# Attention in fp32: the weights of a step's two key blocks added before the products with ones

## The reference

```python
scores = jnp.einsum('bhqd,bhkd->bhqk', qn, kn) / jnp.sqrt(jnp.asarray(hd, x.dtype))
scores = jnp.where(causal, scores, jnp.finfo(scores.dtype).min)
w = jax.nn.softmax(scores, axis=-1)
a = jnp.einsum('bhqk,bhkd->bhqd', w, v)
```

## Time and profile before

| | before |
|---|---|
| median of 3 runs | 2315.25 us (2311.72 to 2317.13) |
| the profiled execution, its own time | 2315.28 us |
| its span | 2313.6 us |
| PE busy | 2164.0 us, 94% |
| DVE busy | 1176.7 us, 51% |
| ACT busy | 809.5 us, 35% |
| POOL busy | 734.2 us, 32% |
| mean granted TensorE clock | 0.969 |

### The profile page before, as it was taken

How to read it: one execution, slowest core, us unless ns; L and a number is a source line. 1 busy time by engine, 2 the same in 40 slices (tenths; PEclk the granted TensorE clock), 3 DMA queues, 4 the chain that set the end, 5 groups by cost and what they waited for, 6 DMA issues and landing times. The chain is left out here.

```text
span 2313.6 us, 36853 instructions
## 1 busy us (share of the span) xinstructions
PE 2164.0 (94%) x14056; PEld 1685.2 (73%) x14056; DVE 1176.7 (51%) x2747; ACT 809.5 (35%) x1607; POOL 734.2 (32%) x612
## 2 busy tenths in 40 slices
PE   6999996599999999999697999999999999999998
PEld 3777774377777777776475888888888888888887
DVE  5999997666667676663695222222212212222212
ACT  3333332056665666666485111111111111111111
POOL 1676776212222213222401742222222222222221
PEclk8999998589999999999898999999999999999999
DMA  6122222637566575741785422121111212121111
GB/s 237 55 104 96 93 98 109 151 94 165 142 149 158 134 164 129 164 109 49 219 303 188 127 78 69 51 69 55 56 45 51 69 57 71 51 69 55 50 33 55
DMA packets 175604, 244.00 MB, mean 105 GB/s; under 512 B 20604, under 2 KB 99580, under 8 KB 174936
## 3 DMA queue, kind: packets, MB, share of 16 engines
q1 hardware_dynamic: 173176, 235.56, 35.6%
q0 software_dynamic: 1216, 3.16, 0.5%
q10 hardware_dynamic: 1056, 3.15, 0.3%
HBM read 131.69 MB, written 59.26 MB: 83 GB/s over the span
## 5 line engine op out<-in xcount | busy, mean ns | idle before, releaser
L1384 DVE TENSOR_TENSOR f_gu<-f_psU,f_silu 128x512 f32<-128x512 f32 x128 | 88.6, 692 | 705.1 <-PE f_psU L1454 705.1
L1000 ACT ACTIVATE b_probT<-b_psB 128x512 f32<-128x512 f32 (+1 forms) x640 | 317.0, 554 | 171.6 <-PE b_psB L864 169.4
L933 DVE TENSOR_REDUCE b_top<-b_psA 128x2 f32<-128x1024 f32 (+2 forms) x320 | 284.6, 902 | 154.1 <-PE b_psA L841 154.1
L1340 POOL TENSOR_SCALAR f_wd_hi<-f_wd 128x512 fp32r<-128x512 f32 x128 | 84.0, 656 | 712.9 <-PE f_psD L1437 712.9
L1360 ACT ACTIVATE f_silu<-f_psG 128x512 f32<-128x512 f32 x128 | 76.5, 598 | 504.8 <-PE f_psG L1454 504.8
L864 PEld LDWEIGHTS b_psB<-b_stack 98*128 98x128 f32 x1280 | 184.2, 191 | 73.1 <-issue 51.6
L864 PE MATMUL b_psB<-b_stack 98*128 98x256 f32 (+1 forms) x1280 | 219.1, 292 | 6.0 <-ACT b_probT L1000 3.7
L1452 PE MATMUL f_psG<-f_hT_hi,w_hi 128*128 128x512 f32 x512 | 200.2, 391 | 12.2 <-DVE f_hT_lo L1378 12.2
L1355 ACT ACTIVATE f_gu_hi<-f_gu 128x512 fp32r<-128x512 f32 x128 | 80.9, 632 | 364.5 <-DVE f_gu L1384 364.5
L841 PE MATMUL b_psA<-b_stack 96*128 96x512 f32 (+3 forms) x768 | 185.0, 371 | 23.5 <-DMA b_stack<-b_halves 18.3
L1454 PE MATMUL f_psG<-f_hT_lo,w_hi 128*128 128x512 f32 x512 | 199.9, 390 | 0.0
(11 more groups left out here) (175 smaller groups left out, 3997.6 us busy)
## 6 DMA issues: line engine op xcount, KB each, us to landing
b_stack<-b_halves SPq DMA_DIRECT2D x192, 256.0 KB, 4.7
f_wd<-in_wd_t SPq DMA_DIRECT2D x128, 256.0 KB, 2.6
qkv_d<-a_t SPq DMA_DIRECT2D x32, 512.0 KB, 2.7
b_land<-qkv_d SPq DMA_DIRECT2D x32, 512.0 KB, 4.2
a_x<-in_x SPq DMA_DIRECT2D x32, 256.0 KB, 3.3
qkv_d<-a_v SPq DMA_DIRECT2D x32, 256.0 KB, 3.0
b_v<-qkv_d SPq DMA_DIRECT2D x16, 512.0 KB, 7.0
att_d<-b_acc SPq DMA_DIRECT2D x16, 512.0 KB, 3.2
```

Of the source, the lines that this page charges most:

```text
L933: last = dve.tensor_reduce(into, tile[:, :, col:col + whole_blocks * P], AX.X, ALU.max, negate=True)
L1000: act.activation(probT[:, (NW * n + w) % PROBS, j, 0:width], psB[:, i % BANKS, 0:width], ACT.Exp).then_inc(s["expd"], 1)
```

## The change

Five of the six blocks off the diagonal, `PAIRED` = 1, 3, 4, 6 and 8 (not 7), get a new operation `pair`: it adds the two key blocks e = 0 and e = 1 of `probT` into a buffer `pairs` (two deep), two heads to an instruction, so two additions of 128x512. For blocks 1 and 4 POOL does it, in the step in which their exponentials are made. For blocks 3, 6 and 8 (`BY_VECTOR`) DVE does it, first thing in the step after, ahead of that step's maxima. The product with ones of such a block then runs over `pairs`: four products instead of eight, with one wait for the first two heads and one for the last two. `pairs` is free again when the products with ones of two pairs ago are done.

Beside this, POOL's `normalise` now stands ahead of `cut`, `pair` and `high` in its step, and three semaphores are merged into others, with the same meaning.

```diff
+    PAIRED = [w for w, (q, g) in enumerate(BLOCKS) if g != q and w != NW - 3]
+    BY_VECTOR = PAIRED[1::2] + PAIRED[4:]
...
+            def pair(n, w):
+                at = paired_index(n, w)
+                if at >= 2:
+                    before = NW * ((at - 2) // len(PAIRED)) + PAIRED[(at - 2) % len(PAIRED)]
+                    pool.wait_ge(s["summed"], before + 1)
+                for x in range(2):
+                    heads = slice(2 * x, 2 * x + 2)
+                    pool.wait_ge(s["expd"], 4 * (NW * n + w) + 2 * x + 2)
+                    prob = probT[:, (NW * n + w) % PROBS, heads]
+                    pool.tensor_tensor(pairs[:, at % 2, heads], prob[:, :, 0:QW], prob[:, :, QW:W], ALU.add).then_inc(s["paired"], 1)
+
...
             for k in STEPS:
-                if cut_at(k):
-                    cut(*cut_at(k))
-                if prep_at(k):
-                    high(*prep_at(k))
                 n, w = unit(k)
                 if w == 0 and 0 <= n - 3 < NG - 1:
                     normalise(n - 3)
+                if cut_at(k):
+                    cut(*cut_at(k))
+                if pair_at(k) and pair_at(k)[1] not in BY_VECTOR:
+                    pair(*pair_at(k))
+                if prep_at(k):
+                    high(*prep_at(k))
...
+                if summing and w in PAIRED:
+                    at = paired_index(n, w)
+                    for j in range(4):
+                        if j % 2 == 0:
+                            mine = [x for x in PAIRED if (x in BY_VECTOR) == (w in BY_VECTOR)]
+                            count = 2 * (len(mine) * n + mine.index(w))
+                            pe.wait_ge(s["paired_v" if w in BY_VECTOR else "paired"], count + j // 2 + 1)
+                        mm = pe.matmul(out[j * HD:(j + 1) * HD], ones[:], pairs[:, at % 2, j],
+                                       start=False, stop=False, skip_group_check=True)
+                    mm.then_inc(s["summed"], 1)
+                    return
...
             for k in STEPS:
+                if vector_pair_at(k):
+                    pair(*vector_pair_at(k))
                 if score_at(k):
```

More of the change, by code:

```diff
@@ L181, in qkv_stage @@
         wmod_in = [sem(f"wmod_in{n}") for n in range(2)]
-        cleared, widened, silu_done = sem("cleared"), sem("widened"), sem("silu_done")
+        cleared, silu_done = sem("cleared"), sem("silu_done")
         small_mm, small_act, small_dve, bias_in = sem("small_mm"), sem("small_act"), sem("small_dve"), sem("bias_in")
@@ L302, in _ @@
             dve.wait_ge(shift_in, 32)
-            dve.tensor_copy(shifts_wide[:, :, :, 0:1], shifts[:].unsqueeze(3)).then_inc(widened, 1)
+            dve.tensor_copy(shifts_wide[:, :, :, 0:1], shifts[:].unsqueeze(3)).then_inc(s["consts"], 1)
             def scale_first():
@@ L518, in _ @@
             pe.wait_ge(w_in, 32)
-            pe.wait_ge(widened, 1)
+            pe.wait_ge(s["consts"], 7)
             for k in range(KC):
@@ L627, in attention_stage, with paired_index @@
     DIAGONAL = [w for w, (q, g) in enumerate(BLOCKS) if g == q]
+    PAIRED = [w for w, (q, g) in enumerate(BLOCKS) if g != q and w != NW - 3]
+    BY_VECTOR = PAIRED[1::2] + PAIRED[4:]
+    def paired_index(n, w):
+        return len(PAIRED) * n + PAIRED.index(w)
     def cut_at(k):
@@ L631, in cut_at, with pair_at, vector_pair_at @@
         return at if at and at[1] in DIAGONAL else None
+    def pair_at(k):
+        at = shift_at(k)
+        return at if at and at[1] in PAIRED else None
+    def vector_pair_at(k):
+        at = weigh_at(k)
+        return at if at and at[1] in BY_VECTOR else None
     def take_at(k):
@@ L674, in attention_stage @@
         probT = sb("b_probT", [P, PROBS, 4, W])
+        pairs = sb("b_pairs", [P, 2, 4, QW])
         acc = sb("b_acc", [P, 2, 2, C])
@@ L682, in attention_stage @@
         names = ("mask_in ln_ready whole ident_ready consts k_ones qk_in v_in turned hi_done lo_done scored maxed peaks_ready "
-                 "peaks_turned peaks_copied peaks_in shifted expd cut weighed summed taken sums_out few_in inverted few_out "
-                 "wide_in scaled end_inverted end_scaled").split()
+                 "peaks_turned peaks_copied peaks_in shifted expd cut paired paired_v weighed summed taken sums_out few_in inverted few_out "
+                 "wide_in scaled ended").split()
         s = {n: sem("b_" + n) for n in names}
@@ L734, in store @@
                 else:
-                    sp.wait_ge(s["end_scaled"], 1)
+                    sp.wait_ge(s["ended"], NQ + 1)
                 dst = scratch["att"][n // GROUPS * TB:(n // GROUPS + 1) * TB, :, n % GROUPS, :].rearrange("t p q -> p t q")
@@ L953, in gather, with pair @@
                 dve.tensor_tensor(peaks[:, 4 * TB:8 * TB].bitcast(F32R), least[:], hi, ALU.subtract).then_inc(s["peaks_ready"], 1)
+            def pair(n, w):
+                at = paired_index(n, w)
+                if at >= 2:
+                    before = NW * ((at - 2) // len(PAIRED)) + PAIRED[(at - 2) % len(PAIRED)]
+                    dve.wait_ge(s["summed"], before + 1)
+                for x in range(2):
+                    heads = slice(2 * x, 2 * x + 2)
+                    dve.wait_ge(s["expd"], 4 * (NW * n + w) + 2 * x + 2)
+                    prob = probT[:, (NW * n + w) % PROBS, heads]
+                    dve.tensor_tensor(pairs[:, at % 2, heads], prob[:, :, 0:QW], prob[:, :, QW:W], ALU.add).then_inc(s["paired_v"], 1)
             def finish(q):
@@ L958, in finish @@
                 dve.wait_ge(s["taken"], NQ * n + q + 1)
-                dve.reciprocal(sums[:, n % 2, cols], sums[:, n % 2, cols]).then_inc(s["end_inverted"], 1)
-                dve.wait_ge(s["end_inverted"], q + 1)
+                dve.reciprocal(sums[:, n % 2, cols], sums[:, n % 2, cols]).then_inc(s["ended"], 1)
+                dve.wait_ge(s["ended"], q + 1)
                 mul = dve.tensor_tensor(att[:, n % 2, cols], att[:, n % 2, cols], sums[:, n % 2, cols], ALU.mult)
                 if q == NQ - 1:
-                    mul.then_inc(s["end_scaled"], 1)
+                    mul.then_inc(s["ended"], 1)
             for k in STEPS:
+                if vector_pair_at(k):
+                    pair(*vector_pair_at(k))
                 if score_at(k):
```

## The result

| | before | changed |
|---|---|---|
| median | 2314.89 us (4 runs, 2311.72 to 2317.13) | 2281.28 us (4 runs, 2278.27 to 2282.69) |
| ratio | | 0.9854, 95% interval 0.9837 to 0.9871 |
| span of the profiled execution | 2313.6 us | 2276.5 us |
| one unit of attention | 40.11 us | 37.89 us |

The change makes the kernel 33.6 us faster; 2287.6 us was forecast, 2278 to 2304 the range. The two profiled executions differ by 37.1 us in span: attention accounts for 34.6 of it (from the first product with ones to the last, 479.9 to 1103.3 us before and 476.9 to 1065.7 after), the rest lies in the other stages. There it is most likely the spread of single executions, since nearly the same instructions brought the first product with ones at 476.9 to 479.9 us in five profiles. So I go by attention, and there by units and steps.

A forecast was written before the change was run, and what follows sets the result against it. PE's stream was taken to bound attention. A gain of 35.2 us less 1.5 (step 7), 2.8 (ACT) and 3.2 (meetings) gave 27.7 us off 2315.3: 2287.6 us, range 2278 to 2304.

The forecast's parts named there:

- PE is the bound, and a product loses 0.44 us: Attention's products with ones: each paired block drops 256 columns, 0.44 us; five in each of 16 units, 35.2 us.
- the far end of 39.2 us: Products with ones: half of the whole group saved, 80 x 0.49 us, if the four saved weight loads count too.
- The waits cost nothing: The two new waits on PE for the sums: 0, of bounds 0 to 0.1 us each.
- POOL's additions: 0, DVE's 1.3 us a pair: POOL's additions, blocks 1 and 4: cost 0. DVE's, blocks 3, 6 and 8: 1.3 us a pair, in idle time before maxima.
- The 0.1 us in step 7: PE's second scoring item in step 7 waits for late maxima of step 6: 0.1 us per unit, 1.5 us in 15 units.
- ACT in step 2: Last shifted head in step 2 needs the first exponential's bank: PE waits about 0.2 us in 14 units, 2.8 us.
- Meetings of DVE and POOL: Normalise on POOL goes ahead of block 8's second DVE addition: 0.8 us stall of `prepare` in four early units, 3.2 us.
- the three terms of loss: Subtracted from the 35.2 us gain: step 7 1.5 us, ACT in step 2 2.8 us, meetings 3.2 us.
- the first rival: Attention: nothing is lost, 2280 us, down to 2276 with the far end; chance 0.20.
- The slower rival: A DVE addition costs POOL's 1.28 us, a pair 2.56; steps 7, 0 and 1 stall: 2337 us; chance 0.08.
- No change: Paired products: a wait between heads 1 and 2 makes four products take two turns, as long as before: 2315 us; chance 0.06.

The follow-up runs named there:

- six blocks: The changed kernel with block 7 added too, by GpSimd in step 9, its product with ones in step 0 made short: 2276.61 us, ratio 0.9847.
- full products: The changed kernel with the additions on both engines and PE's waits kept, but all eight full products with ones run: 2320.28 us, ratio 1.002.

## Why the prediction was right

The way and the size were right, 27.7 us forecast and 33.6 measured, and the time fell into the range, 6.3 us below the point. By its steps:

- **PE is the bound, and a product loses 0.44 us.** 0.43 to 0.44 in steps 4, 6, 7, 9 and 1. The short product takes 0.55 us from start to start; 0.54 was forecast. So the cost goes by columns (0.98, 0.76 and 0.55 us for 512, 384 and 256 of each head), and the far end of 39.2 us is out.
- **The waits cost nothing.** Confirmed: products without additions and waits have the same unit, 37.89 us.
- **POOL's additions: 0, DVE's 1.3 us a pair.** 1.23 to 1.29. Right, and so were the places. The 0.1 us in step 7 was too much: the maxima of step 6 are 0.3 late instead of 0.5, and nothing is lost, 1.5 us in the sum.
- **ACT in step 2: 0.2 us forecast, 0.08 measured.** I had given the first exponential 0.45 us; the four took 1.62 in all. That PE comes early is the cause: with all additions on POOL, where step 1 was held up, step 2 is 2.97 us as before. And step 3 gave 0.09 back, which I had not looked for. Before, `low` reached DVE 0.01 us after the cut had started and took 2.16 us; now PE and with it the maxima are 0.4 earlier, `low` gets in first and takes 1.22, and the cut waits instead (2.15 us), with time to spare. The run with all additions on POOL shows that step 3 goes with this: it is 4.87 us in the seven units where that `low` took 2.16, and 4.79 or 4.80 in the four where it took 1.22 behind the same step 2. In the sum 2.8 us, in truth nothing.
- **Meetings of DVE and POOL: 3.2 us forecast, 0.3 measured.** The mechanism was there, in one unit instead of four. The term that was mis-sized is where the pair of block 8 stands: 3.7 to 5.0 us into step 0, not 4.0 to 5.3, since the maxima of step 0 were late by 0.2 and not by 0.5; while normalise came at 4.2 to 6.4. In six other units it came in the second addition, and POOL waited. The price of one varies with the moment it comes: 0.3 us here, 0.8 with six blocks, up to 1.15 with full products; 0.8 was forecast.

Together the three terms of loss were 7.2 us too pessimistic (1.5, 2.8 and 2.9), and the gross gain 0.6 too optimistic (34.6 us, 80 x 0.432). That makes 34.3 us; the attention of the two profiled executions gained 34.6, the medians 33.6. So the first rival (nothing is lost, 2280 us) is the better description of the result.

- **The slower rival** was the right kind of mechanism, with the wrong price. With a pair at 2.56 us I had 2337 us; the run with doubled additions took 2354. I had the room of each place, but neither the other engine's instruction right behind it nor the second turn of a split product (units of 42.1 us, 2.0 above before, where 1.5 was forecast), nor the clock that fell in four units.
- **No change**, the third rival, needed the two halves of a product to come apart. In the changed kernel they don't: from 500 to 1025 us PE's list of waits has a single one, of 0.2 us, for the maxima. Where they did, with block 3's additions doubled, two heads took as long as four, 0.56 us, just as the rival has it.

## What to carry over

Where one engine's stream is full from end to end, moving columns off it pays in full, and the question is only where the new work stands on the others. Go place by place: how long is the engine idle just there, what stands behind, and what does the neighbour engine do in that microsecond. The same five additions gave 2281 us and 2301 us, and the same six 2276 and 2304, with nothing changed but who does them and what they are queued behind.

A step that waits for transfers does not belong ahead of work that is ready: `normalise` behind the addition instead of ahead of it was worth 17 us.

A gain shifts everything that is timed by transfers against everything that is timed by PE. It moved normalise out of the way here; a stall moves it back, and then one lost microsecond brings a second. A longer wait can bring a third, when TensorE's clock falls behind it. So look at the granted clock of single units before putting all of a loss down to waits.

## What the runs showed of the hardware

When both engines have two instructions with two inputs in SBUF ready, VectorE and GpSimd take turns: two of 1.28 us and two of 0.65 us took 2.97 us on GpSimd and 3.47 us on VectorE, from first start to last end of each (666.50 to 670.02, in the run with full products). Neither gets both of its instructions through first. The Trainium skill ("SBUF — State Buffer", Who interferes with whom) says that the one that starts first has the ports for its whole instruction and the other is blocked; the trace agrees, with 1.77 us for an addition that takes 0.68 alone. VectorE's reductions out of PSUM kept their length beside GpSimd's normalise (0.43 us for 256 columns, at 580.00 beside it and at 749.64 before the change with GpSimd idle), as the same section says.

Weight loads for column groups over the same rows stay hidden: from 384 to 256 columns of each head a product saves 0.21 us with half as many loads, from 512 to 384 it saves 0.22 with as many. The rule of the Trainium skill ("TensorE: Matmul & The Clock Gate", Part 3) that was weighed in the prediction, which would have had them count, is not borne out in this kernel.

The products of the four heads, in four groups of 32 columns, ran side by side: four heads took 0.55 us (601.09 to 601.64), two heads alone 0.56 (612.07 to 612.63, block 3 doubled). Where a wait of 0.46 us fell between the halves, it cost a second turn.

TensorE's granted clock can fall in the middle of a busy stage: to 0.50 for some 6 us behind a wait of 1.90 us (636 to 642, all additions doubled) and one of 2.10 us (862 to 868, all additions on POOL), to 0.58 and 0.57 for some 4 us behind 0.65 us (778 to 782, block 3 doubled), where most waits of that size left it at 1.00.
